# An adaLN block with attention and a mixture of experts: shared tiles stored among whole ones, and the two tile maps computed and turned at other visits

## The reference

```python
def reference(x, w_in, b_in, w_out, b_out, router_w, w1, b1, w2, b2, c, wmod):
    ...
    h = _layernorm(x, axis=-1) * (1 + ca) + sa
    x = x + ga * _L0_attn_ref(h, ...)                  # 32 x 256 x 128 tokens, 16 heads
    h = _layernorm(x, axis=-1) * (1 + cb) + sb
    x = x + gb * _L0_ffn_ref(h, router_w, w1, b1, w2, b2)
    return x

def _L0_ffn_ref(h, router_w, w1, b1, w2, b2):          # 14 experts, 128 -> 256 -> 128
    logits = x @ router_w
    assignments = jnp.argmax(logits, axis=-1)
    probs = jax.nn.softmax(logits, axis=-1)
    weights = jnp.take_along_axis(probs, assignments[:, None], axis=1)[:, 0]
    hid = jax.nn.gelu(jnp.einsum('nd,edf->nef', x, w1) + b1, approximate=False)
    all_out = jnp.einsum('nef,efd->ned', hid, w2) + b2
    sel = jnp.take_along_axis(all_out, assignments[:, None, None], axis=1)[:, 0, :]
    return (sel * weights[:, None]).reshape(Bb, Ss, Dd)
```

## Time and profile before

| | |
|---|---|
| median of 3 runs | 622.87 us (620.76 to 623.65) |
| profiled execution, its own time | 624.31 us |
| span from its first to its last instruction | 622.5 us |
| busy: PE, DVE, ACT, POOL | 471.1, 564.3, 542.3, 483.0 us |
| share of the span | 76%, 91%, 87%, 78% |
| first stage | to about 500 us |
| second stage | from there to 622.5 us |

### The profile page before, as it was taken

One profiled execution on the slowest core, in us unless ns is written; L12 is line 12 of the kernel. 1 busy time (PEld: TensorE's weight loads), 2 busy tenths in 40 slices (PEclk: granted clock), 3 DMA queues, 4 the chain that ended last, 5 costly groups with the idle time before them and its releaser, 6 DMA issues.

```text
span 622.5 us, 11883 instructions
## 1 busy us (share of the span) xinstructions
PE 471.1 (76%) x2535; PEld 265.6 (43%) x2537; DVE 564.3 (91%) x1432; ACT 542.3 (87%) x2310; POOL 483.0 (78%) x642
## 2 busy tenths in 40 slices
PE   5457877877887787788787887788776876799990
PEld 2113333433333343343343443343332465688980
DVE  5899999999999999999999999999999787878983
ACT  2599999999999999999999999999999745467760
POOL 4476777998899899999988999898887754567544
PEclk9555567566556756655556556655655589999996
DMA  6465454555555545554555456665553128857741
GB/s 190 106 185 149 135 137 129 151 148 150 148 155 147 157 143 150 144 153 141 140 141 145 135 148 178 181 169 155 152 168 127 51 97 222 274 176 203 230 124 34
DMA packets 77071, 94.41 MB, mean 152 GB/s; under 512 B 12806, under 2 KB 60710, under 8 KB 76998
## 3 DMA queue, kind: packets, MB, share of 16 engines
q1 hardware_dynamic: 68842, 75.69, 45.0%
q0 software_dynamic: 6144, 16.82, 7.2%
q10 hardware_dynamic: 2015, 1.15, 0.7%
HBM read 58.41 MB, written 35.20 MB: 150 GB/s over the span
## 4 chain that ended last, share of the span: by engine, by line
ACT 47%; POOL 18%; DVE 14%; issue 8%; PE 6%; DMA 4%; SPq 1%; DVEq 1%; ACTq 1%; POOLq 0%
ACT scores L887 46%; POOL table L804 3%; DVE neg_max L1339 3%; POOL xhat L753 2%; POOL rstd L736 2%; DVE y_biased_s L1910 2%; POOL rest L545 1%; POOL parts L548 1%; PE scores L1167 1%; DMA x_s<-table 1%; POOL out_dram L862 1%; PE scores L1176 1%; POOL h_scaled L776 1%; DMA table<-rows,place_i 1%; SPq L556 1%
## 5 line engine op out<-in xcount | busy, mean ns | idle before, releaser
L887 ACT ACTIVATE scores<-scores,neg_max 128x256 f32<-128x256 f32 x1024 | 467.5, 838 | 11.1 <-DVE neg_max L1339 11.0
L887 ACT ACTIVATION_READ_ACCUMULATOR scores<-scores,neg_max 128x1 f32 x1024 | 432.2, 599 | 0.0
L1339 DVE TENSOR_REDUCE neg_max<-scores 128x4 f32<-128x1024 f32 x256 | 309.2, 1211 | 7.1 <-PE scores L1019 6.5
L1019 PE MATMUL scores<-k_stack,q_stack 64*128 64x256 bf16 x1024 | 148.3, 388 | 79.0 <-ACT scores L887 68.5
L1019 PEld LDWEIGHTS scores<-k_stack,q_stack 64*128 64x128 bf16 x1024 | 33.9, 106 | 163.7 <-ACT scores L887 118.9
L804 POOL DMA_INDIRECT table<-rows,place_i x64 | 66.1, 1032 | 20.5 <-issue 17.1
L862 POOL DMA_INDIRECT out_dram<-out_room,x_s x51 | 49.8, 976 | 37.3 <-DVE out_room L1923 29.3
L1176 PE MATMUL scores<-w_s,hid 128*128 x308 | 50.5, 287 | 5.1 <-DVE y_biased_s L1910 3.2
L753 POOL TENSOR_SCALAR xhat<-rows,mv,rstd 128x128 f32<-128x128 f32 x60 | 47.5, 794 | 7.1 <-POOL rstd L736 7.1
L1047 PE MATMUL side_a<-w_gated,opt_t 128*128 128x128 f32 x128 | 49.8, 491 | 0.0
L745 POOL TENSOR_SCALAR xhat<-x_s,mv,rstd 128x128 f32<-128x128 f32 x62 | 49.0, 798 | 0.4 <-POOL rstd L736 0.4
(11 more groups left out here) (224 smaller groups left out, 878.7 us busy)
## 6 DMA issues: line engine op xcount, KB each, us to landing
x_s<-table SPq DMA_DIRECT2D x77, 192.5 KB, 3.0
q_stack<-parts_dram SPq DMA_DIRECT2D x192, 64.0 KB, 2.9
parts_dram<-parts SPq DMA_DIRECT2D x31, 384.0 KB
k_stack<-parts_dram SPq DMA_DIRECT2D x186, 64.0 KB, 2.3
mod_b<-mod_rows SPq DMA_DIRECT2D x32, 256.0 KB, 4.4
x_s<-in_x_dram SPq DMA_DIRECT2D x13, 256.0 KB, 5.0
table<-pad_tile SPq DMA_DIRECT2D x15, 192.5 KB
w1x_s<-in_w1x_dram SPq DMA_DIRECT2D x7, 258.0 KB, 4.6
```

The source lines that it names most:

```text
L887: last = act.activation(buf[:, k * L:k * L + L], buf[:, k * L:k * L + L], ACT.Exp, bias=neg_max[:, p, n:n + 1], accum_out=exp_sum[:, p, n: ...
L1019: last = pe.matmul(scores[:, c, at:at + L], q_stack[p][r, g + j, t * P:t * P + P], k_stack[p][r, g + j, :], start=True, stop=True)
L1339: dve.tensor_reduce(to, scores[:, (PAIRS * b.n + i) % RING, :].rearrange("p (e j m) -> p e j m", e=2, j=2), AX_X, ALU.max, negate=True).th ...
```

## The change

Three things. Packed tiles are stored as soon as a bound says that they are complete: `merged_by` now gives min(k + 14, 2k + 2) merges, and `stores()` lists all 64 stores, with packed tile k directly behind the visit whose merge completes it. The packed stores get a semaphore of their own. The 14 functions of the shared map stand one in each step from 12 to 25 of DVE; PE turns the result behind visit 28 (`SHARED_TURNED` = 28) and DVE takes it in step 30. And both turnings on PE stand at the end of their step instead of its beginning: the first map is turned behind the work of step 9, and DVE takes it in step 10.

```diff
-SHARED_AT = 15
-SHARED_TURNED = SHARED_AT + 9
+SHARED_AT = 12
+SHARED_TURNED = SHARED_AT + 16
...
-def merged_by(slot):
-    return slot - WHOLE + E
+def merged_by(k):
+    return min(k + E, 2 * k + 2)
+
+def stores():
+    order, packed = [], 0
+    for q in range(NT):
+        f, v = VISITS[q]
+        if f is not None:
+            order.append((f, None))
+        while packed < PACKED and v is not None and merged_by(packed) == v + 1:
+            order.append((None, packed))
+            packed += 1
+    return order
...
             for s in range(SLOTS):
-                sp.wait_ge(out_stored[s], 16 * len(range(s, T, SLOTS)))
+                sp.wait_ge(out_stored[s], 16 * len(range(s, WHOLE, SLOTS)))
+            sp.wait_ge(packed_stored, 16 * PACKED)
...
-            for n in range(FIRST, T):
-                store(n)
+            for n, k in STORES[FIRST:]:
+                if n is not None:
+                    store(n)
+                else:
+                    store_packed(k)
...
                 if shared_reload(j):
                     load_experts(SHARED_COL + shared_of_visit(j), shared_reload(j))
-                if j == MAP_TURNED:
-                    turn_map()
-                if j == SHARED_TURNED:
-                    turn_shared()
                 if in_range(j):
                     turn_tile(j)
...
                 elif j > 2 * PRIMED:
                     contract(j - AT_W2)
+                if j == MAP_TURNED:
+                    turn_map()
+                if j == SHARED_TURNED:
+                    turn_shared()
...
-                if j == MAP_TURNED:
+                if j == MAP_TURNED + 1:
                     take_map()
...
-                if j == SHARED_AT:
-                    shared_rest()
-                    shared_rest_f()
...
-                if j == SHARED_AT + 7:
-                    shared_edges()
+                steps_shared = (shared_rest, shared_rest_f, shared_places, shared_places_i, shared_split, shared_split_f, shared_spans,
+                                shared_before, shared_bounds, shared_low, shared_high, shared_in, shared_columns, shared_edges)
+                if 0 <= j - SHARED_AT < len(steps_shared):
+                    steps_shared[j - SHARED_AT]()
```

More of the change, by code:

```diff
@@ L244, in shared_reload @@
     return min(SLOTS, SHARED - v) if v is not None and v % SLOTS == 0 else 0
-def merged_by(slot):
-    return slot - WHOLE + E
+def merged_by(k):
[10 more added lines that the diff above has]
+    return order
+STORES = stores()
+assert len(STORES) == T
 def early_slots(b):
@@ L508, in build_adaln_attention_moe @@
         merged = sem("merged")
+        packed_stored = sem("packed_stored")
         rows_loaded = [sem(f"rows_loaded{s}") for s in range(SLOTS)]
@@ L853, in store, with store_packed @@
             def store(n):
[L855 to L858, removed]
-                else:
[L860 to L865, removed]
-            for n in range(FIRST, T):
-                store(n)
+                q = AT_VISIT[n]
+                pool.wait_ge(out_ready, q + 1)
+                pool.indirect_dma_start(out_rows, bass.IndirectOffsetOnAxis(ap=rows_in[q % SLOTS][:, ID:ROW].bitcast(I32), axis=0),
+                                        out_s[q % SLOTS][:, :], None).then_inc(out_stored[n % SLOTS], 16)
+            def store_packed(k):
+                pool.wait_ge(merged, merged_by(k))
+                pool.indirect_dma_start(out_rows, bass.IndirectOffsetOnAxis(ap=packed[:, k, D:OUT], axis=0),
+                                        packed[:, k, 0:D].bitcast(F32), None).then_inc(packed_stored, 16)
+            over_batches(iteration, drain)
+            for n, k in STORES[FIRST:]:
+                if n is not None:
+                    store(n)
+                else:
+                    store_packed(k)
         @block.scalar
```

## The result

The changed kernel took **619.18 us** (median of 11 runs, 615.50 to 621.21) against 622.87 us (11 runs, 620.76 to 624.72): a ratio of 0.9925, 95% interval 0.9902 to 0.9947. (Ratios and their intervals are estimated from the single runs, so a ratio need not be the quotient of the two medians, 0.9941 here.) That is 3.69 us less where 5.10 were forecast: faster, and inside the range, but 1.4 us short. Taken twice more on other occasions, the same kernel gave 0.9958 (0.9936 to 0.9980) and 0.9941 (0.9922 to 0.9961), so a gain of 2.8 to 3.8 us in the medians. The gain is there; its parts are not those of the sum.

A forecast was written before the change was run, and what follows sets the result against it. Bound by POOL's late stores at the end, DVE's shared-map steps and POOL's store pace in the middle. 2.86 + 2.51 + 0.72 − 0.99 = 5.10 us off 622.87 gives 617.77, range 615.8 to 621.2.

The forecast's parts named there:

- The end: Last packed stores on POOL: only one store is left when DVE's last merge ends, a gain of 2.86 us.
- The shared map: Visits 12 to 25: steps spread one a visit bring DVE's visit 26 earlier, a gain of 2.51 us.
- the price of the steps: Shared map's steps on DVE with what surrounds them: 14.25 us of visits 15 to 22 less eight bare visits, 6.81 us.
- The upper bound: Most the shared map's spreading could gain: 2.55 us of PE's wait plus 0.99 for one slow visit.
- The load wait of visit 48: PE's wait for visit 48's load at 571.19 goes because POOL's stores begin earlier, a gain of 0.72 us.
- The first map: Turned behind visit 9, which runs in PE's wait for the map at 517.10: 0 on the path.
- The clock: PE's longer idling lowers its clock over visits 12 and 13: a loss of 0.99 us, bounds 0 and 1.98.
- The rival that the clock holds: PE's clock does not fall over visits 12 and 13, so 0.99 us is not lost: 616.78 us, chance 0.23.
- The interleaved six: Six packed stores between whole ones on POOL, each delaying a whole store 1.51 us: cost 0 taken.
- the spare time of the loads: Slack of visit 61's load behind visit 45's store: 1.64 us to spare, of which 1.51 are used.
- The rival of whole stores held up: Loads of visits 57 to 76 come late, each of six packed stores costing 1.51 us: 626.83 us, chance 0.08.
- The middle is not POOL's: Judges the rival that POOL's 1.26 us a store sets the pace from visit 22, losing 2.51 and 0.72: 621.00, chance 0.14.

The follow-up runs named there:

- both maps alone: Changed kernel with the order of stores of the kernel before, leaving only the two maps' changes: 622.70 us, ratio 0.9982.
- shared map alone: Kernel before with only the shared map's steps one a visit and its turning behind visit 28: 620.78 us, ratio 0.9944.
- first map ahead again: Changed kernel with the first map turned ahead of visit 9 again and taken by DVE a visit earlier: 618.36 us, ratio 0.9913.

## Why the prediction was right, and where its sum was off

**The end: right.** 2.75 us against 2.86. No backlog was left; a store starts 0.38 us after the last merge's end instead of 0.27.

**The shared map: right in kind, too small.** The 2.51 us are 3.4 to 3.6: A went from 30.19 to 26.61 where the clock holds. The prediction's own stretch, from the first bias to step 26, went from 22.14 us to 18.53 (both maps alone), 18.76 (shared map alone) and 18.57 (first map ahead again). The step that failed is the price of the steps, 6.81 us, read from elapsed time; with the other terms of that sum as they stand, 5.7 to 5.9 are left for them. The view by stretches for DVE (busy time behind the length): visits 15 to 22 of before, then the whole stretch before and with the first map ahead again:

```profile
527.16:541.41 14.25, 13.22 (x68) 1.00 0.93 277
524.14:546.28 22.14, 18.88 (x90) 0.92 0.89 271
...
524.86:543.43 18.57, 17.46 (x89) 1.00 0.94 300
```

DVE idled 14.25 − 13.22 = 1.03 us in the eight visits. Take that off, and the sum gives 2.51 + 1.03 = 3.54, the right size. But that is not the whole reason: over the whole stretch idle time shrank by 3.26 − 1.11 = 2.15 us and busy time by 18.88 − 17.46 = 1.42, of which the copies of weights, which here too ran into stores of POOL before, are 0.41 (4.08 against 3.67 us for 13). What made up the rest no run separates. The upper bound, 3.54 by another way, was the better value.

**The load wait of visit 48: wrong, 0 to 0.1 instead of 0.72.** It is gone (PE turned that tile at 569.22 without a wait), but next to nothing was won by it. From product 26 to product 52, which takes in the turn of visit 48 and its product, it is 29.36 us before, 29.29 with the shared map alone and 29.26 with both maps alone: DVE sets the pace there, and PE's wait lay in PE's lead. The step that failed was to count a wait of PE in a stretch where the other engine is the bound.

**The first map: right as a term, 0.** Visit 12 turned at the same time (522.82, 522.77), with a longer wait ahead of it.

**The clock: right in kind and place, half the size.** Foreseen between 520 and 527 over two visits with 0.99 us on the path, it fell in each of the four profiles of after, over up to three and a half visits, and cost 2.0, just past the upper bound of 1.98. I let one of the excesses hide behind DVE's steps. In the trace of after, DVE's product of visit 10 stands 6.50 us behind the turn of visit 12 (529.32, 522.82); in the three kernels with the new shared map, no matmuls and no fall it is 4.06 to 4.28, so none hid. How long a fall lasts was read from the nearest one, of two visits. The rival that the clock holds, at 0.23, was not seen in after; with the map ahead it is what the traces show from visit 12 on.

**The interleaved six: wrong, 0.6 to 1.1 us instead of 0.** The cover that I named, the spare time of the loads, held in after. PE waits there in front of visits 50 and 67, but in front of both PE loads experts into registers, and visit 67 was waited for as long before (before, then after):

```profile
592.62 0.30 PE L1159 MATMUL scores<-ident_s,x_s 128*128 128x128 f32 x1 [0.69 <-issue]
...
591.99 0.30 PE L1182 MATMUL scores<-ident_s,x_s 128*128 128x128 f32 x1 [0.72 <-DMA x_s<-table]
```

The cost came on an engine that I hadn't looked at, through copies that meet POOL's stores. "Below nothing it cannot be" was right, and "0" was not. The rival of whole stores held up (1.51 us each) came in one of the four profiles of after, and small: in the second, the late load of visit 65 cost DVE 0.43 us.

**The middle is not POOL's.** The 3.4 us of the shared map alone arrived whole at the last merge, so that rival falls too.

The sum with measured sizes: 2.75 for the end, 30.19 − 26.61 = 3.58 for the shared map, 2.02 lost to the clock and 0.86 to the copies, 3.45 us together; the medians of after gave 2.76 to 3.84. One gain had been taken 1.07 us too small, and four terms 0.11 + 0.72 + 1.03 + 0.86 = 2.72 us too well; the difference, 1.65, is what the sum of 5.10 had too much. That the total stayed inside the range owes something to errors of both signs. The range itself ends at 621.2, 0.2 us above the rival that it is said to go by, with no term for that.

**Left open.** Five of the 11 first runs of after took 615.5 to 617.6 us, and six 619.2 to 621.2. All four profiles of it (621.21, 621.03, 620.03 and 620.06 us) show the fall. The groups' means lie 3.5 us apart. That the clock held in the lower group could account for 2.0 of that, but it has no profile, and none of the 14 later runs of the same kernel came under 619.6 us.

## What to carry to other kernels

When work is pulled into one wait, look at the next wait of the same engine: here visit 9 filled a wait that cost nothing, the wait behind it grew, and the clock fell behind that. Price moved work by busy time rather than by elapsed time, and count a wait only on the engine that sets the pace of its stretch. And when transfers are issued from POOL between others, look at what DVE does in the same microsecond: the kernel with the lowest median beside after interleaves only three stores and leaves the first map where it was.

## What the runs showed of the hardware

- A DVE copy of 128x258 f32 that began 0.55 to 0.62 us after the start of a POOL indirect store took 0.44 to 0.51 us instead of 0.29 (83 of 84 such copies in the 14 profiles); begun 0.63 to 0.72 after it, it took 0.43 to 0.32 (105 of 108). Begun earlier than 0.50 after it, none of 261 took more than 0.32, and later than 0.77 444 of 451 took 0.30 or less. So a slow copy ended some 1.05 us after the store's start.
- Waits of PE of 2.50, 2.98, 3.18, 3.40 and 3.88 us ahead of visit 12 were followed by a granted clock of 0.50 (1.2 GHz); waits of 2.22, 2.28 and 2.70 us were not. Waits of 1.72, 1.94, 1.94 and 1.95 us for the first map were followed by 0.50 as well, and others of 1.72, 3.18 and 3.24 us for it were not. What PE had done before them differed, so no bound on the wait alone follows.
